# Attention in a float32 kernel: one 32-column product per head, denominators compacted and spread by DMA, multiplied on GpSimd

## The reference

```python
qkv = x @ W_qkv.T
q_p = elu(einsum('bhnd,hdf->bhnf', q, proj)) + 1.0
k_p = elu(einsum('bhnd,hdf->bhnf', k, proj)) + 1.0
kv = einsum('bhnf,bhnd->bhfd', k_p, v)
attn = einsum('bhnf,bhfd->bhnd', q_p, kv)
k_sum = k_p.sum(axis=2)
z = 1.0 / (einsum('bhnf,bhf->bhn', q_p, k_sum) + 1e-08)
attn = attn * z[..., None]
...
return attn @ W_out.T + b_out
```

## Time and profile before

| | |
|---|---|
| median of 3 runs | 817.26 us (813.1 to 818.62) |
| profiled execution | 814.0 us, span 812.2 us |
| attention phase, up to the first tile's product | 348.7 us |
| expert phase | the rest |
| PE busy over the span | 92% |
| DVE busy over the span | 69% |
| ACT, GpSimd busy over the span | 58%, 31% |
| granted TensorE clock, mean | 0.98 of full |

### The profile page before, as it was taken

How to read it: one execution, slowest core, us unless ns; L and a number is a source line. 1 busy time by engine, 2 the same in 40 slices (tenths; PEclk the granted TensorE clock), 3 DMA queues, 4 the chain that set the end, 5 groups by cost and what they waited for, 6 DMA issues and landing times.

```text
span 812.2 us, 19839 instructions
## 1 busy us (share of the span) xinstructions
PE 746.2 (92%) x6226; PEld 627.9 (77%) x6227; DVE 558.2 (69%) x1370; ACT 467.8 (58%) x968; POOL 255.5 (31%) x192
## 2 busy tenths in 40 slices
PE   2699999999999998799999999999999999988993
PEld 2584748474747474469999999999989999988992
DVE  8889999999999989876446464446464444646442
ACT  2466666656656566566466755457565456765542
POOL 6032525343434435112222233222233222223222
PEclk9899999999999999999999999999999999999997
DMA  6674463636363646643344322253533225352331
GB/s 158 176 199 114 132 188 100 195 92 196 91 203 84 181 103 172 234 168 74 54 133 119 73 47 50 47 138 52 138 52 49 51 43 140 53 136 47 54 53 20
DMA packets 71806, 89.57 MB, mean 110 GB/s; under 512 B 11424, under 2 KB 55136, under 8 KB 71648
## 3 DMA queue, kind: packets, MB, share of 16 engines
q1 hardware_dynamic: 57520, 70.06, 31.2%
q0 software_dynamic: 13728, 18.62, 13.2%
q10 hardware_dynamic: 528, 0.52, 0.2%
HBM read 38.71 MB, written 25.30 MB: 79 GB/s over the span
## 4 chain that ended last, share of the span: by engine, by line
PE 52%; DVE 19%; DMA 17%; issue 8%; ACT 2%; DVEq 1%; POOLq 0%; POOL 0%; ACTq 0%
DMA out<-ysb,icur 16%; PE F L449 5%; PE F L450 5%; PE F L451 5%; PE NUM L449 4%; PE NUM L451 4%; PE NUM L450 4%; DVE kp L1192 3%; PE F L527 3%; PE WK L449 3%; PE WK L450 2%; PE WK L451 2%; PE DEN L451 2%; PE DEN L449 2%; PE DEN L450 2%
## 5 line engine op out<-in xcount | busy, mean ns | idle before, releaser
L965 ACT ACTIVATE h<-F,b1c 128x256 f32<-128x256 f32 x296 | 131.7, 467 | 175.5 <-PE F L451 175.4
L1542 POOL DMA_INDIRECT out<-ysb,icur x74 | 118.8, 1605 | 335.1 <-DVE ysb L1390 189.8
L879 ACT ACTIVATE e_ring<-F 128x512 f32<-128x512 f32 x256 | 147.7, 608 | 56.0 <-PE F L527 35.6
L1373 DVE TENSOR_TENSOR hl<-h,hh 128x512 fp32r<-128x512 f32 x148 | 100.2, 690 | 107.2 <-ACT hh L969 105.8
L449 PE MATMUL F<-gxh,wh 128*128 128x256 f32 x592 | 169.0, 285 | 4.8 <-issue 4.8
L450 PE MATMUL F<-gxl,wh 128*128 128x256 f32 x592 | 167.7, 283 | 0.0
L451 PE MATMUL F<-gxh,wl 128*128 128x256 f32 x592 | 167.7, 283 | 0.0
L449 PEld LDWEIGHTS F<-gxh,wh 128*128 128x128 f32 x592 | 113.7, 192 | 8.1 <-issue 8.1
L450 PEld LDWEIGHTS F<-gxl,wh 128*128 128x128 f32 x592 | 113.7, 192 | 0.2 <-issue 0.2
L451 PEld LDWEIGHTS F<-gxh,wl 128*128 128x128 f32 x592 | 113.7, 192 | 0.0
L1490 POOL DMA_INDIRECT xg<-rows,slots x64 | 63.4, 991 | 143.7 <-issue 143.7
(11 more groups left out here) (194 smaller groups left out, 1492.5 us busy)
## 6 DMA issues: line engine op xcount, KB each, us to landing
wraw<-L_ffn_W SPq DMA_DIRECT2D x16, 1024.0 KB, 7.9
grow<-xg SPq DMA_DIRECT2D x38, 272.0 KB
Sk<-kdh SPq DMA_DIRECT2D x64, 128.0 KB, 2.3
Sq<-qdh SPq DMA_DIRECT2D x64, 128.0 KB
xin<-L_attn_x SPq DMA_DIRECT2D x8, 512.0 KB
Sk<-kdl SPq DMA_DIRECT2D x32, 128.0 KB, 2.3
Sq<-qdl SPq DMA_DIRECT2D x32, 128.0 KB
xres<-L_attn_x SPq DMA_DIRECT2D x8, 512.0 KB, 4.1
```

The source lines that it names most:

```text
L879: A(e_ring[:, u % 4, :], F[u % 4][:, :], ACT.Exp, bias=EXP_BIAS, scale=1.0 / DOWN).then_inc(exp_done, 1)
L965: A(h32[:, m, :], F[m % 4][:, 0:T], ACT.Gelu, bias=b1c[:, w, m:m + 1]).then_inc(gelu, 1)
L1373: V.tensor_tensor(hl[:, 2 * q:2 * q + 2, :], h32[:, 2 * q:2 * q + 2, :], f32(hh[:, 2 * q:2 * q + 2, :]), ALU.subtract).then_inc(hl_rdy, 1)
L1542: pool.indirect_dma_start(out, bass.IndirectOffsetOnAxis(icur[:, s, :], 0), ysb[:, s, :], None, bounds_check=last_token, compute_op=ALU.ad ...
```

## The change

Each head now has one set of 32 weight columns, `st_w`: 16 for the numerator and one for the denominator (a plain copy of the transposed state). `attend(b, c)` multiplies four heads into one bank, NUM and DEN in turn, and ACT copies the bank to `att_sb` (`copy_att`). `gather_att` on SP then compacts by DMA: four DMAs bring the denominators as 128 x 64 to `den`, eight bring the numerators to `at`. DVE adds 1e-8 and takes the reciprocals of 128 x 64 at u = 9 and 10. `spread_rec` on SP stores them to DRAM, waits for that store, and reads them back repeated over the partitions by eight DMAs into `rec_bc`. GpSimd multiplies `at` by `rec_bc` (`normalise`) ahead of `at_hi` and `at_lo`. The products of the selection matrix are gone. In the last iteration both stand ahead of `load_raw(0)`. The last batch's projection moves behind tile 0's `ffn2`, and its multiplication stays on DVE.

```diff
+        def gather_att(b):
+            sp.wait_ge(att_rdy, 4 * b + 4)
+            for j in range(4):
+                r = 32 * j
+                sp.dma_start(den[r:r + 32, :],
+                             att_sb[r + HD:r + HD + 1, :, :].rearrange("p c (k t) -> p (c k) t", t=CHUNK)
+                             ).then_inc(den_ld, 16)
+            for j in range(4):
+                for s in range(2):
+                    r = 32 * j
+                    sp.dma_start(at[r + 16 * s:r + 16 * s + HD, :, :],
+                                 att_sb[r:r + HD, s:4:2, :]).then_inc(num_ld, 16)
+        def spread_rec(b):
+            sp.wait_ge(rec_rdy, b + 1)
+            sp.dma_start(rec_rows.rearrange("r (k t) -> (r k) t", t=CHUNK), rec[:, :]).then_inc(rec_st, 16)
+            sp.wait_ge(rec_st, 16 * (b + 1))
+            heads = rec_rows.rearrange("(j g s) t -> j s g t", j=4, s=2)
+            for j in range(4):
+                for s in range(2):
+                    r = 32 * j + 16 * s
+                    sp.dma_start(rec_bc[r:r + HD, :, :],
+                                 heads[j, s].unsqueeze(0).to_broadcast([HD, 2, NTOK])).then_inc(rec_ld, 16)
...
             load_x(b + 2)
+            gather_att(b - 1)
+            spread_rec(b - 1)
             stack_k(b + 1)
             store_o(b - 1)
             load_xres(b)
             stack_q(b + 1)
...
+        gather_att(NB - 2)
+        spread_rec(NB - 2)
         sp.wait_ge(f_full, 32 * NB - 16)
         load_raw(0)
...
+        def attend(b, c):
+            if c == 0:
                 pe.wait_ge(state_rdy, b + 1)
-            pe.wait_ge(feat, 32 * b + 20 + 8 * g + 4 * s)
-        def attn_den(b, g, s):
-            attn_wait(b, g, s)
+            else:
+                wait(pe, att_rdy, 4 * b + c - 1)
+            pe.wait_ge(feat, 32 * b + 20 + 4 * c)
             for j in range(4):
-                h = 8 * g + 4 * s + j
-                last = nc.tensor.matmul(DEN[32 * j:32 * j + 32, :], den_w[:, h, :], qp[:, h, :],
-                                        start=g == 0 and s == 0, stop=g == 1 and s == 1,
-                                        skip_group_check=True)
-            if g == 1 and s == 1:
-                last.then_inc(den_done, 1)
-        def attn_num(b, g, s):
-            attn_wait(b, g, s)
-            if s == 0:
-                wait(pe, num_rdy, 2 * b + g)
-            for j in range(4):
-                h = 8 * g + 4 * s + j
-                last = nc.tensor.matmul(NUM[32 * j:32 * j + 32, :], num_w[:, h, :], qp[:, h, :],
-                                        start=s == 0, stop=s == 1)
-            if s == 1:
-                last.then_inc(attn_done, 1)
...
-                    attn_den(b - 1, 1, 0)
-                if u == 1 and not first:
-                    attn_num(b - 1, 1, 0)
                 if u == 3 and not first:
-                    attn_den(b - 1, 1, 1)
-                if u == 5 and not first:
-                    attn_num(b - 1, 1, 1)
+                    attend(b - 1, 3)
...
-                if u == 27:
+                    project(b - 1, 1, PROJ_BANK[1])
+                if u == 26:
                     if first:
                         pe.wait_ge(v_rdy, NT * b + 7)
                     else:
                         pe.wait_ge(o_rdy, 2 * b + 1)
-                    attn_num(b, 0, 0)
-                if u == 26:
-                    attn_den(b, 0, 0)
+                    attend(b, 0)
                 if u == 28:
-                    attn_den(b, 0, 1)
-                if u == 29:
-                    attn_num(b, 0, 1)
+                    attend(b, 1)
+                if u == 31:
+                    attend(b, 2)
...
+            if m == 3:
+                attend(NB - 1, 3)
             ffn1(0, 0, m)
-            if m == 1:
-                attn_den(NB - 1, 1, 1)
-                attn_num(NB - 1, 1, 0)
-                attn_num(NB - 1, 1, 1)
-            if m == 4:
-                pe.wait_ge(state_rdy, NB)
-                spread(NB - 1, 0)
-                pe.wait_ge(num_rdy, 2 * NB)
-                spread(NB - 1, 1)
-            if m == 6:
-                pe.wait_ge(at_rdy, 2 * NB)
-                project(NB - 1, 0)
-                project(NB - 1, 1)
-        pe.wait_ge(o_rdy, 2 * NB + 2)
         rows_T(1)
+        pe.wait_ge(att_rdy, 4 * NB)
         for s in range(SUB):
             ffn2(0, 0, s)
+        pe.wait_ge(gxl_rdy, 2)
+        for i in range(2):
+            project(NB - 1, i, LAST_PROJ_BANK[i])
...
+        def copy_att(b, c):
+            act.wait_ge(attn_done, 4 * b + c + 1)
+            if c == 0:
+                wait(act, num_ld, NUM_INC * b)
+                wait(act, den_ld, DEN_INC * b)
+            A(att_sb[:, c, :], ATT_BANK[c][:, :], ACT.Copy).then_inc(att_rdy, 1)
         def state(b):
             act.wait_ge(state_full, b + 1)
-            wait(act, attn_done, 2 * b)
-            st = STATE[:, :].rearrange("p (h c) -> p h c", c=32)
-            for s in range(2):
-                A(num_w[:, :, :].rearrange("p (g s j) c -> p g s j c", s=2, j=4)[:, :, s, :, 16 * s:16 * s + HD],
-                  st.rearrange("p (g s j) c -> p g s j c", s=2, j=4)[:, :, s, :, 0:HD], ACT.Copy, scale=1.0 / DOWN)
-            for c in range(4):
-                last = A(den_w[:, 4 * c:4 * c + 4, c:c + 1], st[:, 4 * c:4 * c + 4, HD:HD + 1], ACT.Copy, scale=1.0 / DOWN)
-            last.then_inc(state_rdy, 1)
...
         def denominators(b):
-            dve.wait_ge(den_done, b + 1)
-            V.tensor_scalar(den_sb[:, :], DEN[:, :], 1e-8 * DOWN, None, ALU.add).then_inc(den_read, 1)
-        def reciprocals(b, q):
-            dve.wait_ge(den_read, b + 1)
-            cols = slice(q * P, (q + 1) * P)
-            last = V.reciprocal(rec_sb[:, cols], den_sb[:, cols])
-            if q == 3:
-                last.then_inc(rec_rdy, 1)
-        def normalise(b, g):
-            dve.wait_ge(num_rdy, 2 * b + g + 1)
-            dve.wait_ge(spread_full, 2 * b + g + 1)
-            V.tensor_tensor(at[:, g, :], num_sb[:, g, :], SPREAD_BANK[g][:, :], ALU.mult).then_inc(at_rdy, 1)
+            dve.wait_ge(den_ld, DEN_INC * (b + 1))
+            V.tensor_scalar(dsum[:, :], den[:, :], 1e-8 * DOWN, None, ALU.add).then_inc(dsum_rdy, 1)
+        def reciprocals(b):
+            dve.wait_ge(dsum_rdy, b + 1)
+            V.reciprocal(rec[:, :], dsum[:, :]).then_inc(rec_rdy, 1)
...
-                    if u == 4:
+                    if u == 9:
                         denominators(b - 1)
-                    if u in (5, 7, 9, 10):
-                        reciprocals(b - 1, (5, 7, 9, 10).index(u))
-                    if u in (16, 17):
-                        normalise(b - 1, u - 16)
+                    if u == 10:
+                        reciprocals(b - 1)
...
+        dve.wait_ge(num_ld, NUM_INC * NB)
+        dve.wait_ge(rec_ld, NUM_INC * NB)
         for g in range(2):
-            normalise(NB - 1, g)
+            V.tensor_tensor(at[:, g, :], at[:, g, :], rec_bc[:, g, :], ALU.mult).then_inc(at_rdy, 1)
...
+        def normalise(b, g):
+            if g == 0:
+                pool.wait_ge(num_ld, NUM_INC * (b + 1))
+                pool.wait_ge(rec_ld, NUM_INC * (b + 1))
+            nc.gpsimd.tensor_tensor(at[:, g, :], at[:, g, :], rec_bc[:, g, :], ALU.mult).then_inc(at_rdy, 1)
...
             add_bias(b - 1)
             for g in range(2):
+                normalise(b - 1, g)
+            for g in range(2):
                 at_hi(b - 1, g)
```

More of the change, by code:

```diff
@@ L61, in constants @@
     c[:, C_PAD:C_PAD + SUB] = p[:, None] + P * np.arange(SUB) + TOKENS
-    for g in range(2):
-        for r in range(P):
-            c[32 * (r // 32) + 2 * g + (r % 32) // 16, C_SEL + P * g + r] = 1.0
     return c
@@ L137, in build @@
     kv_sb = sb("kv_sb", [P, 512], F32)
-    num_w = sb("num_w", [P, HEADS, 32], F32)
-    den_w = sb("den_w", [P, HEADS, 32], F32)
+    st_w = sb("st_w", [P, HEADS, 32], F32)
+    den = sb("den", [P, CHUNK], F32)
+    dsum = sb("dsum", [P, CHUNK], F32)
+    rec = sb("rec", [P, CHUNK], F32)
     r_num = place[0]
-    num_sb = sb("num_sb", [P, 2, 512], F32)
-    den_sb = sb("den_sb", [P, 512], F32)
-    rec_sb = sb("rec_sb", [P, 512], F32)
+    att_sb = sb("att_sb", [P, 4, 512], F32)
     at = sb("at", [P, 2, 512], F32)
     ath = sb("ath", [P, 2, 512], F32R)
+    r_atl = place[0]
     atl = sb("atl", [P, 2, 512], F32R)
+    rec_bc = sb_at("rec_bc", [P, 2, 512], F32, r_atl)
     o_sb = sb("o_sb", [P, NT, D], F32)
@@ L535, in kv @@
                 pe.wait_ge(v_rdy, NT * b + NT)
-                wait(pe, den_read, b)
+                wait(pe, att_rdy, 4 * b)
             for c in range(4):
@@ L648, in iteration @@
                     kv(b, 2)
-                if u == 17 and not first:
-                    if not last:
-                        pe.wait_ge(qkl_rdy, 4 * b + 6)
-                    else:
-                        pe.wait_ge(pos_read, b + 2)
-                    spread(b - 1, 0)
-                if u == 18 and not first:
```

(60 more changed lines are left out.)

80 lines of the change are left out of this document (39 added, 41 removed).

## The result

The changed kernel takes **864.0 us** (862.73 to 868.23, 4 runs) against 817.07 (813.1 to 818.62, 4 runs) beside it: ratio 1.059, 95% interval 1.054 to 1.064. Slower, as forecast, inside the range, and 20 us above the 844 forecast. The profiled execution took 862.73.

The account below looks back on a forecast made before the run. PE and DVE bound the kernel before; after the change a chain through SP and GpSimd would. 814.0 + 19.6 to the first tile + 6.0 in it + 2.5 for scatters = 842.1, stated as 844 us, range 812 to 866.

Parts of the forecast that it names:

- The chain through SP and GpSimd: Attention loop: gather, store, spread, multiplication and split follow one another and start `project` 32.4 us after `stack_q` starts; iteration 42.2 us.
- S: The start of `stack_q` on SP's queue, the end of the iteration's last unit on PE; the forecast counts from it.
- the clock behind the wait: Behind PE's wait before `project`: granted clock of 0.5; about 3 us at half speed cost 1.5 us.
- DVE held by `den` at u = 9: Sign that the forecast is wrong: PE's wait before `project` ended by DVE waiting for the denominators; about 1 us thought possible.
- The rival in which issues hardly count: Loop bound by PE and DVE alone at 35.3 us per iteration: 776 to 780 us in all; chance 0.05.
- Late landings: Rival: new transfers land late, both DRAM landings 4.1 and issues 0.64 us, +4.7 per chain; 880, half of it 863; chance 0.11.
- PE's wait: In front of `project` in every iteration: PE waits some 6.7 us for the chain, its busy time down to 32.5.
- the first tile: Last batch's gather, store, spread, multiplication, split and projection inside it: 27.5 us instead of 21.5, +6.0.
- The last iteration: Both new blocks ahead of `load_raw(0)`: last `project` of the loop 36.4 us after `stack_q` starts, against 28.1.
- The end: After the second tile starts: the first scatter waits for the last store, 3.7 us later, of which 2.5 kept.
- the sum of 842.1: Forecast for an execution like the profiled one: 814.0 + 19.6 + 6.0 + 2.5 us.

Follow-up runs that it names:

- The doubled issues: The changed kernel with each batch's four denominator DMAs issued a second time into a spare tile that nobody reads: 882.1 us, ratio 1.080 to the kernel before.
- the bystanders: The kernel before with 21 DMAs of the change's patterns added per iteration in SP's loop, no compute engine waiting for them: 817.5 us against 817.8, ratio 1.000.
- the changed order: The changed kernel with the last two of eight `at` DMAs issued behind the store of the reciprocals instead of ahead: 856.2 us, ratio 1.052 to the kernel before.

## Why the prediction was right, and what was mis-sized

**Right: the mechanism and the loop.** The chain through SP and GpSimd sets `project`: S + 32.6 for a forecast 32.4 (31.8 to 33.6 over the six iterations); PE waits there in every iteration; the iteration is 42.65 us for a forecast 42.2; the clock behind the wait is at 0.50. That the sum came out within 0.2 us is in part luck, since the parts were off in both directions. The first `den` starts 0.6 us late and the twelve issues of `den` and `at` take 8.0 us for 6.9 (0.63 and 0.68 each for 0.58). The store and its wait take 2.3 for 2.6, the spread up to GpSimd's start 5.4 for 6.2 (0.45 each for 0.52), GpSimd and the semaphore 7.7 for 8.1. The doubled issues, the bystanders and the changed order show this chain as the cause. One of the prediction's signs against it, DVE held by `den` at u = 9, was there in three of six iterations, 2.3 us in all; the wait of PE covered it. The rival in which issues hardly count, with the Trainium skill's "usually small relative to the DMA itself" ("DMA: Bandwidth & Descriptors", section "Issuing engines are not separate DMA queues") beside it, is out here: 2.42 us of issuing cost 2.1 us per iteration. The same 21 DMAs as bystanders cost nothing, so what decides is who waits at the end of the queue. Late landings are out as well: `rec_bc` and the store landed in some 2 us with the DMA engines at 0.63.

**Sizes that were off without harm.** PE's wait was 4.2 us on average (4.6 in the iteration shown), not 6.7, because PE itself took 36.25 us of busy time for the forecast 32.5: part of it at half clock, also at the start of the iteration, which the prediction didn't have. DVE was busy 35.85, not 33.1; the last section tells where 2.2 of these 2.8 us come from.

**The term that was mis-sized is the first tile: +6.0 forecast, +18.3 measured.** The prediction followed the last batch's own chain (gather, store, spread, multiply, split) and asked only when its projection can start. It didn't ask what else SP's queue holds behind the two moved blocks: the row load of the second tile, for which PE waits in front of `ffn2`. In the prediction's terms: 27.5 us for the tile, 39.9 measured, and of the difference the load moved ahead gives back 12.5. With it the tile takes 27.4 us, and the execution 10 us less.

**Smaller ones.** The last iteration was +10.8 for +8.3: `load_raw(0)` is issued at S + 23.1 instead of 21.4, and `at_hi` waits on ACT behind the first weight copy. The end was +6.2 for +2.5, and mostly for another reason than given: the scatters' later start was seen (417.82), but 4.0 of the 6.2 are the same products at a lower clock. Why the clock falls a few times more in this phase than in the kernel before was not tested; the traces show only that a few short waits of PE are longer. The five differences (1.0, 2.5, 0.8, 12.3, 3.7) make 20.4 of the 20.6 us between the sum of 842.1 and the profiled execution of 862.7.

## What to carry to other kernels

Cost a chain of small DMAs by the issues on its queue and by whoever stands at the end of it, not by bytes: 21 of them cost nothing as bystanders. With a projection behind them they made the iteration 2.9 us longer, although by the forecast DVE had 4.5 us less to do in it and PE 5.7. When blocks are put into an in-order queue, list everything that stands behind them in every phase; here the rows of the next tile were missing from that list, and moving their load was worth 10 us. Work taken from TensorE can cost the clock in the stretch that it is taken from: three useless products put back there were worth 1.2 us per iteration.

## What the runs showed of the hardware that wasn't expected

**DVE waits for GpSimd.** In the changed kernel three tiny operations of DVE fall beside GpSimd's six operations. Their groups in the loop, 66 to 303 us, one of the kernel before and then the three of the changed one (the other two take 171 and 182 ns in the kernel before):

```profile
L1122 DVE COPY cum<-cum 128x8 f32<-128x8 f32 x6 | 1.0, 172 | 0.2
```

```profile
L1107 DVE COPY cum<-cum 128x8 f32<-128x8 f32 x5 | 5.0, 990 | 0.2
L1071 DVE TENSOR_SCALAR rbits<-var 128x4 int32<-128x4 int32 x5 | 4.6, 917 | 0.2
L1105 DVE TENSOR_TENSOR lg<-lraw,br_bc 128x32 f32<-128x32 f32 x5 | 3.9, 770 | 0.0
```

In DVE's timeline the first two of one iteration:

```profile
224.56 1.17 DVE L1107 COPY cum<-cum 128x8 f32<-128x8 f32 x1
...
226.03 1.03 DVE L1071 TENSOR_SCALAR rbits<-var 128x4 int32<-128x4 int32 x1
```

They end at 225.73 and 227.06, as GpSimd's operations change (the last `atl` from 225.78 to 227.04). The features, which read PSUM and one SBUF tile, keep their 0.68 us beside the same GpSimd operations. It is 2.2 us of DVE per iteration (2.68 for 0.53), here hidden behind the wait for `atl`; with the multiplication on DVE and one GpSimd pair left, the copy and the second of them take 0.17 again, the third 0.49. The Trainium skill, "GPSIMD Engine Reference", section "1. Specifications", has the two engines share SBUF interfaces, with contention for DVE instructions in a two-port mode or with two SBUF inputs; by that rule the third of them, with two SBUF inputs, would wait and the features wouldn't, and the trace agrees. The other two have one SBUF input each. They would wait if they run in a two-port mode, which no view here shows; the trace shows only that they wait.

**A granted clock of 0.50 without a pause.** In the kernel with the multiplication on DVE the clock fell to 0.50 in a stretch where PE was busy for 4.55 of 5 us, behind one with 3.94. PE's longest pause in the two was 0.8 us.
